# The cosine attention's opening for batch 0 moved between the pieces of the first attention's later batches

## What is computed

```python
x = x + mla(layernorm(x))        # 16 heads, latent keys, rope, causal softmax
x = x + ffn(layernorm(x))        # one 256x256 product, tanh of the row's norm
x = x + cosine(layernorm(x))     # 16 heads, q and k scaled to unit length, softmax, layernorm of the output
x = x + ffn(layernorm(x))
x = x + gla(layernorm(x))        # gated linear attention, a scan over rows
x = x + workspace(x)             # top-4 rows per slot, twice
x = x + lora_attention(layernorm(x))
x = x + workspace(x)
# ffn:    out = (n @ weight) * scale; v = norm(out)
#         out *= tanh(v) / (v + eps);  out *= min(0.99 / norm(out), 1)
# cosine: q = l2norm(16 * (n @ Wq));  k = l2norm(n @ Wk);  softmax(16 * q k^T) v
```

## Time and profile before

| | us |
|---|---|
| median of three runs (lowest, highest) | 2289.26 (2286.37, 2296.61) |
| the profiled execution, its own time | 2289.46 |
| its span in the profile | 2287.4 |
| busy: TensorE, VectorE, ScalarE, GpSimd | 1990.9, 1040.1, 797.9, 514.7 |
| granted clock of TensorE, mean | 0.942 |

### The profile page before, as it was taken

How to read it: one execution, slowest core, us unless ns; L and a number is a source line. 1 busy time by engine, 2 the same in 40 slices (tenths; PEclk the granted TensorE clock), 3 DMA queues, 4 the chain that set the end, 5 groups by cost and what they waited for, 6 DMA issues and landing times. The chain is left out here.

```text
span 2287.4 us, 29147 instructions
## 1 busy us (share of the span) xinstructions
PE 1990.9 (87%) x11104; PEld 1248.0 (55%) x11104; DVE 1040.1 (45%) x2250; ACT 797.9 (35%) x1757; POOL 514.7 (22%) x617
## 2 busy tenths in 40 slices
PE   6999999999489999999999999668867779999776
PEld 4556566656256766676667667522224444455443
DVE  4554545454322333333333322358764466546443
ACT  2543434453133323332332333123312325445332
POOL 2332222231111011101010110025441135442210
PEclk9999999999699999999999999889978879999897
DMA  6000000000100000000000000020000000000001
GB/s 253 1 1 1 1 1 1 1 1 1 32 1 1 1 1 1 1 1 1 1 1 1 1 1 1 1 66 0 0 1 1 1 0 1 1 1 2 1 1 38
DMA packets 9768, 23.95 MB, mean 10 GB/s; under 512 B 2448, under 2 KB 6304, under 8 KB 8864
## 3 DMA queue, kind: packets, MB, share of 16 engines
q1 hardware_dynamic: 8336, 18.92, 2.3%
q10 hardware_dynamic: 1296, 3.18, 0.4%
HBM read 20.00 MB, written 2.10 MB: 10 GB/s over the span
## 5 line engine op out<-in xcount | busy, mean ns | idle before, releaser
L1170 PEld LDWEIGHTS cos_ps<-cos_vx,cos_probs 128*128 128x128 f32 x2048 | 238.4, 191 | 33.6 <-issue 28.7
L1170 PE MATMUL cos_ps<-cos_vx,cos_probs 128*128 128x129 f32 x2048 | 239.5, 274 | 4.2 <-DVE cos_on L867 4.2
L1161 PE MATMUL cos_ps<-cos_qT,cos_kT 128*128 128x512 f32 x512 | 232.0, 597 | 1.4 <-ACT cos_qT L1023 1.4
L1052 ACT ACTIVATE cos_probs<-cos_ps 128x512 f32<-128x512 f32 x256 | 150.9, 598 | 162.7 <-PE cos_ps L1161 161.6
L366 ACT ACTIVATE probs<-sc,nmax 128x512 f32<-128x512 f32 (+3 forms) x256 | 132.4, 524 | 191.1 <-DVE nmax L229 189.0
L967 POOL TENSOR_TENSOR cos_qrs<-cos_qse,neg_half 128x4 f32<-128x4 f32 x64 | 64.4, 1007 | 510.5 <-DVE cos_qse L849 510.5
L473 PE MATMUL sc<-kT,qT 128*128 128x512 f32 (+3 forms) x512 | 174.0, 462 | 3.9 <-DVE probsT L241 2.5
L1161 PEld LDWEIGHTS cos_ps<-cos_qT,cos_kT 128*128 128x128 f32 x512 | 94.9, 192 | 97.9 <-issue 94.6
L2475 DVE TENSOR_REDUCE cos_wq<-tail_ps 128x2 f32<-128x1024 f32 (+3 forms) x128 | 101.7, 823 | 84.4 <-PE tail_ps L2706 83.3
L847 DVE TENSOR_REDUCE cos_qss<-cos_qsq 128x4 f32<-128x512 f32 x64 | 43.9, 686 | 208.4 <-ACT cos_qsq L1031 208.4
L446 PE MATMUL pq<-xnT,wap 128*128 128x512 f32 x256 | 130.3, 633 | 4.3 <-DVE swp L221 3.9
(11 more groups left out here) (366 smaller groups left out, 3398.4 us busy)
## 6 DMA issues: line engine op xcount, KB each, us to landing
onT<-in_mla_wqT SPq DMA_DIRECT2D x1, 2048.0 KB, 9.2
mla_wo<-in_mla_wo SPq DMA_DIRECT2D x1, 2048.0 KB, 19.4
cos_wq<-in_cos_wq SPq DMA_DIRECT2D x1, 2048.0 KB, 25.5
cos_wout<-in_cos_wout SPq DMA_DIRECT2D x1, 2048.0 KB, 29.8
out<-x SPq DMA_DIRECT2D x4, 512.0 KB, 2.9
x<-in_x SPq DMA_DIRECT2D x1, 1536.0 KB, 14.6
wq_pe<-in_mla_wq_pe ACTq DMA_DIRECT2D x1, 1024.0 KB, 14.2
x<-in_x SPq DMA_DIRECT2D x1, 512.0 KB, 4.6
```

Of the source, the lines that this page charges most:

```text
L1052: act.activation(probs[:, n % 2, kj, :], ps[:, kj, :], ACT.Exp).then_inc(s["e_done"], 1)
L1161: pe.matmul(ps[:, kj, :], kT[:, b % 2, kj * P:(kj + 1) * P], qT[:, hq % 2, h % 4, :], start=True, stop=True).then_inc(s["s_ready"], 1)
L1170: last = pe.matmul(po[:, qi // 2, qi % 2, :], probs[:, n % 2, kj, qi * P:(qi + 1) * P], vx[:, b % 2, kj, :], start=(kj == 0), stop=(kj == ...
```

## The change

1. The opening of batch 0 of the cosine stage is taken out of that stage (its planner, all four engine programs) and made inside the first attention, as 19 pieces in a table of slots, `LEAD_AT`. A slot is a pair (b, p); the piece stands on TensorE at the end of the pair, in the bank `pq` or `po`. Its work on VectorE, GpSimd and ScalarE stands at the end of the pair in their programs too (`lead_vector`, `lead_roots`, `lead["scalar"]`). Each root stands one slot or more behind its sum. There are 19 more semaphores.
2. The first attention's own roots move from p = 1 to p = 2 and from p = 5 to p = 6, and `scale_keys` moves from the end of p = 5 into p = 6, between the first `copy_turned` and the reciprocal.
3. The cosine queries, rows, keys and values live in buffers that both stages see; the folded weights of the first attention and some of the LoRA stage's buffers share them. `cos_wout` (2 MB) and `cos_gout` are loaded with the late loads, and waited for before their first use.
4. In the last stages the fillers grow from 20 to 70 and from 48 to 88, 28 are added in the second workspace, and the LoRA attention gets its own. GpSimd's clearing of slots now waits until VectorE has written the LoRA stage's first rows.

The diff, cut to its core:

```diff
+LEAD_UNITS = 5
+LEAD_AT = {(1, 2): ((("rows", "f", 0), "pq"), (("rows", "f", 1), "po")),
+           (1, 3): ((("prod", "f", 0), "po"),), (1, 4): ((("prod", "f", 1), "po"),),
+           (2, 2): ((("rows", "l", 0), "pq"), (("rows", "l", 1), "po")),
+           (2, 3): ((("kv", "l", 0), "po"),), (2, 4): ((("kv", "l", 1), "po"),),
+           (2, 5): ((("unit", "q", 0), "po"),), (2, 6): ((("unit", "q", 1), "po"),),
+           (3, 1): ((("unit", "q", 2), "pq"), (("turn", "q", 0), "po")),
...
+           (3, 4): ((("turn", "q", 2), "po"),), (3, 5): ((("turn", "q", 3), "po"),), (3, 6): ((("turn", "q", 4), "po"),)}
...
+    def vector(dve, b, p):
...
+        if at == (1, 0):
+            row_stats(dve)
+        elif at == (1, 1):
+            dve.wait_ge(s["lead_rstd"], 1)
+            norm_rows(dve, 0)
+        elif at == (1, 5):
+            scale_weights(dve, 0)
+        elif at == (1, 6):
+            scale_weights(dve, 1)
+        elif at == (1, 7):
+            finish_ffn(dve)
+            row_stats(dve)
...
+        elif at == (3, 4):
+            scale_queries(dve, 3)
+            sum_queries(dve, 4)
...
@@ mla_attention, vector
                     copy_turned(n, 0)
+                    if p == 6 and b + 1 < B:
+                        scale_keys(b + 1)
                     dve.wait_ge(s["e_ready"], 6 * n + 6)
...
                             keys_values(b + 1, pq[:, :])
-                            scale_keys(b + 1)
+                    lead_vector(b, p)
@@ mla_attention, gpsimd
-                        if p == 1:
+                        if p == 2:
                             power(0, "var_ready", "rstd_ready", b + 1)
-                        if p == 5:
+                        if p == 6:
                             power(1, "kvar_ready", "krstd_ready", b + 1)
+                    lead_roots(b, p)
@@ mla_attention, tensor
+                    for key, at in LEAD_AT.get((b, p), ()):
+                        if at == "pq":
+                            pe.wait_ge(s["qa_copied"], n + 2)
+                        else:
+                            pe.wait_ge(s["o_done"], n)
+                        lead["tensor"](pe, key, at)
@@ cosine_attention, tensor
-                for key in cos_ffn("f", 0):
-                    fill(key)
-                pe.wait_ge(s["scaled_w"], 1)
-                for key in COS_LATENT:
-                    fill(key)
-                for u in range(COS_OPENING):
-                    project(0, u)
...
@@ last stages
+            if early > 0 and r == 0 and b >= early:
+                keep_busy(28, WS_TURN_BANKS[b][0])
...
-                keep_busy(20, 3)
+                keep_busy(70, 3)
             else:
-                keep_busy(48, 1)
+                keep_busy(88, 1)
...
+LORA_FILLERS = {("rows", 0, 0): 44, ("turn", 0, "q"): 24, ("rows", 1, 0): 24,
+                ("attend", B * LORA_GROUPS - 1, None): 14, ("out", B * LORA_GROUPS - 1, None): 14, ("on", B - 1, 0): 16,
+                ("y", B - 1, 0): 14}
...
         def clear_slots():
+            pool.wait_ge(s["xn_ready"], 1)
```

More of the change, by code:

```diff
@@ L81, with lead_counts @@
 MLA_TURN_BANKS = ((0,), (1, 3), (2,))
+LEAD_UNITS = 5
+LEAD_AT = {(1, 2): ((("rows", "f", 0), "pq"), (("rows", "f", 1), "po")),
[8 rows of a table added]
+LEAD_BY_VECTOR = ("prod", "kv")
+LEAD_SEMS = ("lead_filled", "lead_by_v", "lead_by_a", "lead_var", "lead_rstd", "lead_xn", "lead_n2", "lead_norm", "lead_tanh",
+             "lead_var2", "lead_rstd2", "lead_k_var", "lead_k_rstd", "lead_kn", "lead_q_sq", "lead_q_var", "lead_q_rstd",
+             "lead_qn", "lead_scaled")
+def lead_counts():
+    filled, emptied, last = {}, {}, {}
+    count = {"lead_by_v": 0, "lead_by_a": 0}
+    for slot in sorted(LEAD_AT):
+        for key, at in LEAD_AT[slot]:
+            who = "lead_by_v" if key[0] in LEAD_BY_VECTOR else "lead_by_a"
+            count[who] += 1
+            filled[key] = len(filled) + 1
+            emptied[key] = (who, count[who])
+            last[(at,) + slot] = emptied[key]
+    return filled, emptied, last
@@ L243, in copy_turned, with lead_vector @@
                     last.then_inc(s["pt_b"], 1)
+                def lead_vector(b, p):
+                    lead["vector"](dve, b, p)
                 def add_output(b):
@@ L310, in rope, with lead_roots @@
                     pool.drain()
+                def lead_roots(b, p):
+                    lead["roots"](pool, b, p)
                 pool.memset(g["neg_half"][:, :], -0.5)
@@ L401, in _ @@
                             copy_keys(b + 1, p - 6, pq[:, :])
+                    lead["scalar"](act, b, p)
                 copy_sums(PAIRS - 1)
@@ L450, in wait_for_piece @@
                 def wait_for_piece(b, p):
+                    lead["free"](pe, "pq", b, p)
                     if p == 0 and b > 0:
@@ L492, in spread_sums @@
                     pe.wait_ge(s["rl_wide"], m + 1)
+                    lead["free"](pe, "po", *divmod(m, MLA_PAIRS))
                     if 1 <= m <= 4:
@@ L616, in cos_ffn @@
     return [("rows", kind, t, 0), ("rows", kind, t, 1), ("prod", kind, t, 0), ("prod", kind, t, 1)]
-COS_LATENT = [("rows", "l", 0, 0), ("rows", "l", 0, 1), ("kv", "l", 0, 0), ("kv", "l", 0, 1), ("keys", "l", 0, 0)]
 def cos_plan():
@@ L653, in project @@
         take(("project", b, u), (at,), ("qn_ready",))
-    for n, key in enumerate(cos_ffn("f", 0) + COS_LATENT):
-        piece(key, n % 4)
-    for u in range(COS_OPENING):
-        project(0, u, 4 + u % 3)
-        if u > 0:
-            piece(("turn", "q", 0, u - 1))
-    piece(("turn", "q", 0, COS_OPENING - 1))
     for b in range(B):
@@ L697, in cosine_attention @@
         xn = k.sb("cos_xn", [P, TI, D])
-        xnT = k.sb("cos_xnT", [P, 2, DC, S])
+        xnT, kT, vx, qT = (g["cos_" + n] for n in ("xnT", "kT", "vx", "qT"))
         fT = k.sb("cos_fT", [P, DC, S])
@@ L729, in cosine_attention @@
         s = {n: k.sem("cos_" + n) for n in names}
-        WEIGHTS = 16 * len(g["early_loads"])
+        LOADED = 16 * len(loads)
         order = []
-        for b in range(-1, B):
-            if b == -1:
-                order += [("f", 0), ("l", 0)]
-                continue
+        for b in range(B):
             order += [("f", b + 1)] if b + 1 < B else []
@@ L971, in root @@
                     pool.tensor_tensor(norm[:, :], n2[:, :], g["pos_half"][:, 0:TI], ALU.pow).then_inc(s["norm_ready"], 1)
-                invert("f", 0)
-                root("f", 0)
-                invert("l", 0)
-                invert_again(0)
-                invert_keys(0)
-                for u in range(COS_OPENING):
-                    invert_queries(0, u)
                 for b in range(B):
@@ L1193, in project_outputs @@
                         last.then_inc(s["y_ready"], 1)
-                pe.wait_ge(g["weights_loaded"], WEIGHTS)
-                for key in cos_ffn("f", 0):
-                    fill(key)
-                pe.wait_ge(s["scaled_w"], 1)
-                for key in COS_LATENT:
-                    fill(key)
-                for u in range(COS_OPENING):
-                    project(0, u)
-                    if u > 0:
-                        fill(("turn", "q", 0, u - 1))
-                fill(("turn", "q", 0, COS_OPENING - 1))
                 for b in range(B):
@@ L2340, in lora_programs @@
     rstd = k.sb("lora_rstd", [P, TI])
-    xn = k.sb("lora_xn", [P, TI, D])
+    early_room = g["lead_room"]
+    at = 0
+    shared = {}
+    for name, n in (("wqk", DC * 2 * D), ("wvo", 2 * DC * 2 * D), ("raw", TI * 2 * D), ("xn", TI * D)):
+        shared[name] = early_room[:, at:at + n]
+        at += n
+    xn = shared["xn"].rearrange("p (i d) -> p i d", i=TI)
     xnT = k.sb("lora_xnT", [P, DC, S])
-    wqk = k.sb("lora_wqk2", [P, DC, 2, D])
-    wvo = k.sb("lora_wvo2", [P, 2, DC, 2, D])
-    raw = k.sb("lora_raw", [P, TI, 2 * D])
+    wqk = shared["wqk"].rearrange("p (c n d) -> p c n d", c=DC, n=2)
+    wvo = shared["wvo"].rearrange("p (b c n d) -> p b c n d", b=2, c=DC, n=2)
+    raw = shared["raw"].rearrange("p (i d) -> p i d", i=TI)
     rot = k.sb("lora_rot", [P, 2, 2 * D])
@@ L2593, in free, with keep_busy @@
                 pe.wait_ge(s[name], n)
+        def keep_busy(n, at):
+            for _ in range(n):
+                pe.matmul(ps[:, at, 0:P], ident_b[:, :], mask_b[:, :], start=True, stop=True)
         def fill(piece):
@@ L2599, in fill @@
             free(piece)
+            keep_busy(LORA_FILLERS.get(piece, 0), at)
             if kind == "rows":
@@ L2965, in build @@
             mla_attention(nc, g, w)
[L2966 removed]
+        late = ["cos_wout", "cos_gout", "gla_wq", "gla_wk", "gla_wgk1", "gla_wv", "gla_wg", "gla_wgk2", "gla_bgk2", "gla_normw", "gla_wo",
                 "gla_sel", "gla_hsum", "gla_same"]
```

305 lines of the change are left out of this document (254 added, 51 removed), and 2 rows, old and new, of the table LEAD_AT.

## The result

The changed kernel takes 2211.19 us in the median (2210.17 to 2212.97, four runs) beside 2289.16 us (2286.37 to 2296.61); the ratio is 0.9644, with a 95% interval of 0.9624 to 0.9664. That is 78 us less, where 80 were forecast. Its profiled execution has a span of 2211.2 us at a mean clock of 0.964.

A forecast was written before the change was run, and what follows sets the result against it. TensorE bounds the first attention, busy 535.6 of 572 us; the cosine opening is an engine-to-engine chain. From 2289.46 us, -68.5 + 1.4 + 5.8 = -61.3, with -19 for the last stages -80.3: 2209 us; forecast 2195 to 2224, 8-in-10 range 2193 to 2240.

The forecast's parts named there:

- The opening: Start of the cosine stage: 68.5 us gone once moved out, less 1.4 us for 19 more semaphores to clear.
- The attention: First attention, which takes in the moved work: grows by 5.8 us in sum.
- pieces on TensorE: First attention: the 19 moved pieces cost their full-speed TensorE time with nothing hiding it, +20.3 us.
- VectorE's lead work: Pair ends of the first attention: the moved opening's VectorE work is mostly hidden, +1.0 us, at most 25.8.
- waits for the widened sums: First attention, `spread_sums`: six of TensorE's seven waits for widened reciprocals go with the later roots, -13.1 us.
- clock dips behind them: First attention: four clock dips of 1.6 us after those waits go too, -6.4 us.
- `scale_keys`: First attention, pair 6: the moved operation delays the turned keys in three batches, +4.0 us, bounds 0 and 3 x 2.0.
- The tail: Workspaces and LoRA attention: more fillers hold the clock and clearing comes later, -19 us, between 0 and 25.
- That the fillers don't hold the clock: Rival for the last stages: they gain nothing or lose up to 6 us, 2228 to 2234 us; chance 0.17.
- That VectorE's work lands on the path: Rival for the first attention: the moved VectorE work costs all 25.8 us instead of 1, 2234 us; chance 0.12.
- The slower side: Rival for the first attention: pieces stall TensorE, 69 us on top, 2297 us, deciding from 3.2 us each; chance 0.03.
- The observation that spoke against the change: First attention: L208 took 0.81 us beside GpSimd's widening, 0.42 without; 13 such meetings could add 5 us, left unsummed.

The follow-up runs named there:

- last stages as before: Changed kernel with the fillers and GpSimd clearing of the last stages put back as in the kernel before; ratio 0.9734 to the kernel before.
- the roots alone: Kernel before with only its first attention's own roots moved one pair later and `scale_keys` moved into pair 6; ratio 0.9938 to the kernel before.
- each piece twice: Changed kernel with the TensorE instructions of each of the 19 pieces issued twice; ratio 0.9724 to the kernel before.
- control: The changed kernel itself, unaltered, run again on the chip of later experiments; median 2210.70 us, ratio 0.9636 to the kernel before.
- tail alone: Kernel before with only the changed kernel's edits to the last stages; ratio 0.9921 to the kernel before.
- VectorE's load: Changed kernel with three useless VectorE operations at the end of every pair of batches 1 to 3; ratio 0.9677 to the kernel before.
- keys early: Changed kernel with `scale_keys` put in front of the first `copy_turned` of pair 6; ratio 0.9641 to the kernel before.
- the first two experiments: Changed kernel with the last stages as before, ratio 0.9734; and kernel before with only the edits to the last stages, ratio 0.9921.

## Why the prediction was right

**The opening** was to give 68.5 us less 1.4 for the semaphores. The first scores follow x by 5.33 us (581.27 for 575.94) where VectorE's first row followed by 4.06: 1.27 us for 19 semaphores (the two rows belong to different engines, so this is a little rough). All 68.5 us went; nothing of them came back in the cosine stage, since from its first scores to the first row of the workspace it is 1062.92 us before and 1062.95 after. No experiment took the opening out by itself, but two of them enclose it: the kernel with the last stages as before stands at -2.66%, the roots alone at -0.62%, and the difference, 47 us, is what the moved opening gives. By the terms it should be 68.5 - 1.3 - 22.4 = 44.8, within the noise of two ratios.

**The attention** was to grow by 5.8 us and grew by 4.3 to its end, or by 5.3 from its first `spread_sums` row. Its terms, with what the experiments gave:

| term | forecast | measured | by |
|---|---|---|---|
| pieces on TensorE | +20.3 | +19.9 | each piece twice |
| VectorE's lead work | +1.0 | +2.5 | changed kernel against the roots alone, 22.4, less 19.9 |
| waits for the widened sums | -13.1 | -13.1 | waits before and after |
| clock dips behind them | -6.4 | -7.2 | roots alone, 17.1 less the waits |
| `scale_keys` | +4.0 | +3.2 | three waits of 1.06 |
| sum | +5.8 | +5.3 | |

The measured terms make up the 5.3 us. That the sum came so near is in part luck: VectorE's term was too small by 1.5 us, while the dips gave back 0.8 more and the keys cost 0.8 less than forecast, and these cancel. VectorE's term was named for the slots (1,5) and (1,7), and that is where the two new waits of 1.32 and 1.11 us stand; they had only been priced at less than half. The releaser was not the maxima, as the prediction said, but ScalarE's copy of the spread sums, which stands behind the exponents that wait for those maxima.

**The tail** was to gain 19 us. The two profiles gave 13.3, the experiment without the edits 18.2 in the profile and 20 by the ratios. The tails of the profiles whose last stages are those of before or those of the changed kernel say more:

| tail, us | kernels |
|---|---|
| without the edits | 580.3 (before), 585.2 (last stages as before), 587.1 (roots alone) |
| with them | 564.0, 567.0 (control, changed kernel), 565.3, 565.7, 565.7, 565.8 (tail alone, pieces twice, VectorE's load, keys early) |

(The kernels that lack one of the edits have 565.7 without the last group's fillers, 569.0 with the clearing at once and 572.5 without the opening's fillers.) The means are 584.2 and 565.6. The edits are worth some 18.6 us, with three profiles on one side that lie 7 us apart; the profile of before was the shortest of the three. So the term was of the right size, though by the two profiles alone it would have looked 6 us too large. Its size is not all insight: the steps added up to 25 us, and the three quarters that made 19 of them came from no row.

The steps can be read in the two profiles. The four selection passages, from L2069 (L2321 after) to the 24 fillers behind it, gained 2.86, 1.33, 1.29 and 2.86 us, 8.3 for the forecast 9.2; L2321 takes 1.93 us four times. From the second of them to the first projection of the LoRA attention 3.9 us more went, of the 4 put there. Its first scores gained 4.3 us (18.7 to 14.4) of the up to 8, with windows still at 0.50 in their middle. The new 28 fillers had some 4 us; the products behind them, L2304 and L2294, take 1.92 and 1.08 us instead of 3.64 and 1.96, 2.6 less. Against that stand 2.9 us for a dip in the LoRA attention (last section) and 2.3 for the fillers of its last group.

**The rivals.** That the fillers don't hold the clock fell with the first two experiments. That VectorE's work lands on the path is true for a pair that is full, not for the mean pair: 34 us of it cost 8.2, and the lead's own work 2.5. The slower side needed 3.2 us for each piece; with VectorE's share it was 22.4 / 19 = 1.2, since every input was there. The observation that spoke against the change, VectorE's rows stretched by GpSimd, does not stand where the prediction read it: the moved L208 (now L504) takes 0.42 us at 273.04, with GpSimd idle. So that row met nothing; how often VectorE was held up elsewhere is not shown, and its 2.5 us hold whatever that cost. The rule that the prediction took from the Trainium skill is also narrower than it was told: it holds for two inputs from SBUF only against a GpSimd operation that reads SBUF, as the widening does.

## What to carry over

In a stage where TensorE is busy 94% of the time, work moved into it costs its full-speed time on TensorE, to within 2%, and it is still worth moving when at its old place it formed a chain that ran at a clock of 0.70 with TensorE busy half of the time. A root or a reduction that another engine needs should stand one step behind what it waits for; that alone gave 17.1 us in the attention, 7.2 of them clock that was lost behind the waits. Judge edits that only hold the clock by several profiles or by ratios, because without them the same instructions took anything from 580 to 587 us. And before a few microseconds are read out of two profiles, find a row from which the same code takes the same time: here the first 50 us moved by up to 4 us, and the 520 behind them by 0.3 or less.

## What the runs showed of the hardware

Two profiles of the very same kernel differ by a clock dip. In the first, TensorE waits 2.41 us in the LoRA attention and the clock then falls for some 7 us:

```profile
1841.00:1844.00 3.00, 0.59 (x10) 0.39 (x10) 3.00 (x4) 1.02 (x1) 2.86 (x5) 1.00 0.00 0
1844.00:1847.00 3.00, 3.00 (x28) 1.12 (x24) 2.45 (x3) 1.62 (x2) 1.97 (x5) 0.75 0.00 0
1847.00:1850.00 3.00, 3.00 (x28) 1.36 (x22) 1.29 (x3) 0.81 (x1) 0.83 (x3) 0.50 0.02 5
```

The kernel before waits longer at that place, 2.90 us, and keeps 1.00:

```profile
1917.00:1920.00 3.00, 0.11 (x4) 0.11 (x4) 3.00 (x5) 0.86 (x1) 2.86 (x5) 1.00 0.02 5
1920.00:1923.00 3.00, 3.00 (x34) 1.21 (x34) 2.72 (x3) 1.62 (x2) 1.38 (x5) 1.00 0.00 0
```

In the control the wait is 2.37 us, and the clock from there on stays at 1.00. The attention of before shows the same in two profiles. TensorE waits 1.93 us at one place, and the clock two microseconds behind it, first in the kernel before, then in the kernel with the tail edits alone, whose attention is the same:

```profile
206.35 0.66 PE L500 MATMUL po<-ident,rlw 128*128 128x128 f32 x4 [1.93 <-POOL rlw L299]
208.00:210.00 2.00, 2.00 (x7) 0.88 (x6) 1.23 (x3) 0.00 (x0) 0.00 (x0) 1.00 0.00 0
```

```profile
206.09 0.66 PE L500 MATMUL po<-ident,rlw 128*128 128x128 f32 x4 [1.93 <-POOL rlw L299]
208.00:210.00 2.00, 2.00 (x3) 0.68 (x3) 0.39 (x1) 0.00 (x0) 0.00 (x0) 0.50 0.00 0
```

At the wait of 2.69 us of batch 0 it is the other way round: 0.50 in the kernel before, 1.00 in the other. Both profiles have four dips in all, and the attention takes 519.2 and 519.5 us. So the length of a wait does not decide alone; what else does was not found. The dip in the LoRA attention costs 2.9 us (the lead over before falls from 76.2 to 73.3 us), and the four runs of the changed kernel lie 2.8 us apart in the first group and 6.2 in the control's, which is of that size.

GpSimd's memset of a slot buffer held up VectorE rows on other data: four rows together took 2.94 us instead of 1.38. Nearly all of it lies in the last of the four, which starts 0.06 us after the memset of 1.89 us and ends 0.14 behind it, while the first three take 0.4 us each:

```profile
1770.68 1.97 DVE L2668 TENSOR_SCALAR lead_room<-x,lora_mv,lora_rstd 128x256 f32<-128x256 f32 x1
```

The Trainium skill, SBUF — State Buffer, section "SBUF: two separate sides", says that VectorE in a two-port mode and a GpSimd operation exclude each other for a whole instruction. By that rule the one row that meets the memset waits for its end and the others pass, and the trace agrees; in which mode VectorE ran no row shows.
